# Message passing on one Trainium2 core: SyncE fetches four of 391 pairs of edge tiles per layer row by row, and the gather ring goes from 20 slots to 16

## What is computed

```python
ew = edge_attr @ edge_w + edge_b
for l in range(3):
    residual = x
    msg = relu(x[src] * ew)
    out = 0
    for i in range(3):                       # three types of edges
        h = segment_sum(msg * (edge_type == i), dst, n)
        out = out + (h * inv_cnt[i]) @ weights[l, i]
    out = out + x @ roots[l] + biases[l]
    x = residual + relu(out)
return layernorm(x0 + x)
```

## Time and profile before

| | us |
|---|---|
| time, median of 3 runs | 3607.24 (3604.1 to 3611.32) |
| the profiled execution's own time | 3611.26 |
| its span, first to last instruction | 3609.5 |
| mean granted TensorE clock | 0.846 of 2.4 GHz |
| busy: PE, DVE, ACT, POOL | 2854.7, 2139.7, 1204.2, 2232.8 |
| layer 0, 1, 2 by their first and last `collect` | 23 to 1232, 1248 to 2421, 2429 to 3597 |

### The profile page before, as it was taken

How to read it: one execution, slowest core, us unless ns; L and a number is a source line. 1 busy time by engine, 2 the same in 40 slices (tenths; PEclk the granted TensorE clock), 3 DMA queues, 4 the chain that set the end, 5 groups by cost and what they waited for, 6 DMA issues and landing times.

```text
span 3609.5 us, 57851 instructions
## 1 busy us (share of the span) xinstructions
PE 2854.7 (79%) x17654; PEld 2646.3 (73%) x17654; DVE 2139.7 (59%) x6079; ACT 1204.2 (33%) x2542; POOL 2232.8 (62%) x2363
## 2 busy tenths in 40 slices
PE   6888887888888777878778778877877777787887
PEld 5777777777777676777777777777777777777776
DVE  5666666666666555555555555555555565656656
ACT  4555555555544322222222222222222222222222
POOL 6666666666666566666666666656666666666664
PEclk8788888898888878788888988887888888888888
DMA  6555555555555444444444444444444444444443
GB/s 171 153 158 152 156 156 158 150 158 160 152 158 158 125 133 122 125 132 122 129 129 125 131 125 131 128 126 130 123 124 126 127 127 128 129 126 127 127 128 97
DMA packets 313363, 491.03 MB, mean 136 GB/s; under 512 B 62115, under 2 KB 200030, under 8 KB 313054
## 3 DMA queue, kind: packets, MB, share of 16 engines
q0 software_dynamic: 112608, 307.65, 30.1%
q1 hardware_dynamic: 199628, 179.45, 16.9%
q10 hardware_dynamic: 818, 0.18, 0.0%
HBM read 429.61 MB, written 57.43 MB: 135 GB/s over the span
## 4 chain that ended last, share of the span: by engine, by line
PE 59%; issue 19%; DVE 11%; another core or an unknown queue 8%; DVEq 3%; DMA 0%; ACT 0%; ACTq 0%
PE bank L973 29%; PE bank L929 16%; PE bank L1018 12%; DVE acc L1195 5%; DVE xg L1369 2%; PE bank L994 1%; DVEq L1339 1%; DVEq L1195 1%; DVE t L1212 1%; DVE t L1251 1%; PE bank L965 0%; DVEq L306 0%; DVE t L1224 0%; DVE S L1154 0%
## 5 line engine op out<-in xcount | busy, mean ns | idle before, releaser
L781 POOL DMA_INDIRECT xg<-x,idx x1540 | 1466.0, 952 | 868.3 <-issue 385.0
L1369 DVE TENSOR_TENSOR xg<-xg,bank 128x512 f32<-128x512 f32 x1170 | 802.7, 686 | 1373.8 <-remote 785.5
L973 PE MATMUL bank<-S,xg 128*128 128x96 f32 x9384 | 1522.8, 313 | 101.6 <-issue 92.6
L973 PEld LDWEIGHTS bank<-S,xg 128*128 128x128 f32 x9384 | 1434.2, 228 | 150.2 <-issue 120.0
L863 ACT ACTIVATE xg<-xg 128x512 f32<-128x512 f32 x1170 | 736.8, 630 | 1855.0 <-issue 1070.1
L929 PE MATMUL bank<-wsb,at 128*128 128x256 f32 x4692 | 1008.8, 344 | 386.7 <-issue 240.9
L929 PEld LDWEIGHTS bank<-wsb,at 128*128 128x128 f32 x4692 | 772.0, 228 | 442.1 <-issue 358.1
L781 POOL DMA_INDIRECT xg<-in_x_dram,idx x782 | 741.7, 948 | 465.3 <-issue 181.4
L1195 DVE TENSOR_TENSOR acc<-acc,bank 128x192 f32 x2346 | 816.1, 348 | 46.0 <-issue 14.8
L1018 PE MATMUL bank<-W,acc 128*128 128x256 f32 (+1 forms) x1764 | 532.8, 422 | 36.0 <-issue 34.3
L1018 PEld LDWEIGHTS bank<-W,acc 128*128 128x128 f32 (+1 forms) x1764 | 399.0, 263 | 51.9 <-issue 40.1
(11 more groups left out here) (72 smaller groups left out, 613.9 us busy)
## 6 DMA issues: line engine op xcount, KB each, us to landing
at<-attr_t SPq DMA_DIRECT2D x585, 128.0 KB
attr_t<-hs SPq DMA_DIRECT2D x196, 128.0 KB
xg<-x,idx POOLq DMA_INDIRECT x1540
hs<-in_attr_q_dram SPq DMA_DIRECT2D x196, 64.0 KB
xg<-in_x_dram,idx POOLq DMA_INDIRECT x782
x<-t SPq DMA_DIRECT2D x96, 128.0 KB
xblk<-x SPq DMA_DIRECT2D x96, 128.0 KB
y<-t SPq DMA_DIRECT2D x94, 128.0 KB
```

The source lines that it names most:

```text
L781: eng.indirect_dma_start(out=xg[:, n % XR, :], out_offset=None, in_=rows_in, in_offset=bass.IndirectOffsetOnAxis(ap=rows_at, axis=0)).then ...
L973: last = eng.matmul(sums_bank(l, q, i)[:, 192 * i + 96 * h:192 * i + 96 * h + 96], xg[:, n % XR, 128 * h:128 * h + 128], S[:, slot(l, 2 * ...
L1369: eng.tensor_tensor(v, v, shared_bank("edges", l, q)[:, :].rearrange("p (i d) -> p i d", i=2), ALU.mult).then_inc(s_m, 1)
```

## The change

In each layer four of the 391 pairs (steps 103, 197, 290 and 384, `by_row`) are not gathered by GpSimd any more. SyncE fetches their rows: it loads eight node numbers at a time from a small table `rown` into registers and issues one DMA of one row for each of the 256 edges of a pair, 1024 a layer, 3072 in all. They are spread evenly over steps 10 to 377 (2.78 rows a step) and stand at the end of each step, behind that step's other DMAs. The rows go to an own buffer `xr` of two pairs (`RB`), the semaphores `s_row` count them, and the first row of a pair waits until the pair that used the buffer before has been summed. To make room the ring `xg` goes from 20 slots to 16: a gather now waits for the pair eight places earlier among those gathered. VectorE waits for one semaphore instead of two at a fetched pair. Nothing is changed in the work of TensorE, VectorE and ScalarE but the places that they read and write.

The core of the diff:

```diff
-    XR, SR, TR, AR = 20, 8, 3, 6
+    XR, SR, TR, AR = 16, 8, 3, 6
...
+    RB, ROW0, ROW1 = 2, 10, 384
+    by_row = [ROW0 + (ROW1 - ROW0) * (i + 1) // 4 for i in range(4)]
...
+        xr = sb("xr", [128, 2 * RB, D])
+        rown = sb("rown", [128, 128], I32)
...
+        def gathered(Q):
+            return Q // NP * (NP - len(by_row)) + Q % NP - sum(p < Q % NP for p in by_row)
+        in_ring = [Q for Q in range(L * NP) if Q % NP not in by_row]
...
+            def load_row_numbers():
+                for i, p in enumerate(by_row):
+                    a = 128 * tile(2 * p)
+                    eng.dma_start(rown[32 * i:32 * i + 2, :], src[a:a + 256].rearrange("(q p) -> q p", q=2)).then_inc(s_rn, 16)
...
+            def fetch_rows(l, a, b):
+                for r in range(a, b):
+                    i, m = divmod(r, 256)
+                    if r == 0 and l == 0:
+                        eng.wait_ge(s_rn, 16 * len(by_row))
+                    if m == 0 and (l or i >= RB):
+                        u = i - RB if i >= RB else i - RB + len(by_row)
+                        eng.wait_ge(s_sc, collected(l if i >= RB else l - 1, by_row[u]))
+                    if m % 8 == 0:
+                        _, vals = nc.values_load_multi_w_load_instructions(
+                            rown[32 * i + m // 128:32 * i + m // 128 + 1, m % 128:m % 128 + 8], engines=[SP], min_val=0, max_val=N - 1,
+                            skip_runtime_bounds_check_because="a source is a node's number")
+                        numbers.update({m % 256 + j: v for j, v in enumerate(vals)})
+                    eng.dma_start(xr[m % 128:m % 128 + 1, 2 * (i % RB) + m // 128, :],
+                                  xs[l][bass.ds(numbers.pop(m), 1), :]).then_inc(s_row[i % RB], 16)
+            def row_of(q):
+                return min(4 * 256, max(0, 4 * 256 * (q - ROW0) // (ROW1 - 6 - ROW0)))
...
                         for k in starting(q, late):
                             store(l, k)
+                        fetch_rows(l, row_of(q), row_of(q + 1))
...
             def gather(l, j):
-                n = l * NT + j
-                if n >= XR:
-                    eng.wait_ge(s_sc, collected(*divmod((n - XR) // 2, NP)))
+                G = gathered(l * NP + j // 2)
+                c = 2 * G + j % 2
+                if c >= XR:
+                    eng.wait_ge(s_sc, collected(*divmod(in_ring[G - XR // 2], NP)))
...
                     for j in range(2 * AHEAD, NT):
-                        gather(l, j)
+                        if j // 2 not in by_row:
+                            gather(l, j)
```

More of the change, by code:

```diff
@@ L209, in gnn_program @@
         s_g = sems("s_g", XR)
+        s_rn = sem("s_rn")
+        s_row = sems("s_row", RB)
         s_e, s_m, s_r, s_S, s_sc, s_acc = (sem(n) for n in ("s_e", "s_m", "s_r", "s_S", "s_sc", "s_acc"))
@@ L268, in reload_step, with rows_of, tile_rows, fetched @@
             return max(2 * g - 5, keep_step(g) + 1)
+        def gathered(Q):
+            return Q // NP * (NP - len(by_row)) + Q % NP - sum(p < Q % NP for p in by_row)
+        in_ring = [Q for Q in range(L * NP) if Q % NP not in by_row]
+        def rows_of(Q):
+            if Q % NP in by_row:
+                c, ring_of = 2 * (by_row.index(Q % NP) % RB), xr
+            else:
+                c, ring_of = 2 * gathered(Q) % XR, xg
+            return ring_of[:, c:c + 2, :]
+        def tile_rows(n):
+            return rows_of(n // 2)[:, n % 2, :]
+        def fetched(l, i):
+            return 16 * 256 * (l * (len(by_row) // RB) + i // RB + 1)
+        def wait_rows(eng, n):
+            l, q = divmod(n // 2, NP)
+            if q in by_row:
+                i = by_row.index(q)
+                eng.wait_ge(s_row[i % RB], fetched(l, i))
+            else:
+                c = 2 * gathered(n // 2) + n % 2
+                eng.wait_ge(s_g[c % XR], 16 * (c // XR + 1))
+        assert all(AHEAD <= p < NP - 1 and tile(2 * p) + 1 < NT - 1 for p in by_row)
         def starting(q, lag):
@@ L686, in _ @@
             keep_attr(0)
+            def load_row_numbers():
+                for i, p in enumerate(by_row):
+                    a = 128 * tile(2 * p)
+                    eng.dma_start(rown[32 * i:32 * i + 2, :], src[a:a + 256].rearrange("(q p) -> q p", q=2)).then_inc(s_rn, 16)
+            SP = mybir.EngineType.SP
+            numbers = {}
+            def fetch_rows(l, a, b):
[15 more added lines that the diff above has]
+                return min(4 * 256, max(0, 4 * 256 * (q - ROW0) // (ROW1 - 6 - ROW0)))
             def load_sources(l):
@@ L722, in fast @@
                                 load_x0(1)
+                        if l == 0 and q == 0:
+                            load_row_numbers()
                         if l == 0 and q in (1, 3, 5, 7):
@@ L781, in gather @@
                 eng.indirect_dma_start(
-                    out=xg[:, n % XR, :], out_offset=None, in_=rows_in,
-                    in_offset=bass.IndirectOffsetOnAxis(ap=rows_at, axis=0)).then_inc(s_g[n % XR], 16)
+                    out=xg[:, c % XR, :], out_offset=None, in_=rows_in,
+                    in_offset=bass.IndirectOffsetOnAxis(ap=rows_at, axis=0)).then_inc(s_g[c % XR], 16)
             eng.wait_ge(s_src0, 32)
@@ L854, in fast @@
                             eng.wait_ge(s_m1, l + 1)
-                            v = xg[:, (2 * Q) % XR, :]
+                            v = tile_rows(2 * Q)
                             eng.activation(v, v, ACT.Relu).then_inc(s_r1, 1)
                             eng.wait_ge(s_m, Q + 1)
-                            v = xg[:, (2 * Q + 1) % XR, :]
+                            v = tile_rows(2 * Q + 1)
                             eng.activation(v, v, ACT.Relu).then_inc(s_r, 1)
@@ L861, in fast @@
                             eng.wait_ge(s_m, Q + 1)
-                            v = xg[:, (2 * Q) % XR:(2 * Q) % XR + 2, :]
+                            v = rows_of(Q)
                             eng.activation(v, v, ACT.Relu).then_inc(s_r, 1)
@@ L973, in collect @@
                         last = eng.matmul(sums_bank(l, q, i)[:, 192 * i + 96 * h:192 * i + 96 * h + 96],
[L974 removed]
+                                          tile_rows(n)[:, 128 * h:128 * h + 128], S[:, slot(l, 2 * q + i), :],
                                           start=True, stop=True)
@@ L1179, in first_rows @@
             def first_rows(l, q):
-                v = xg[:, (2 * (l * NP + q)) % XR:(2 * (l * NP + q)) % XR + 2, :]
+                v = rows_of(l * NP + q)
                 n = AHEAD * (l - 1) + q + 1
@@ L1355, in fast @@
                             for i in range(2):
-                                n = 2 * Q + i
-                                eng.wait_ge(s_g[n % XR], 16 * (n // XR + 1))
-                                v = xg[:, n % XR, :]
+                                wait_rows(eng, 2 * Q + i)
+                                v = tile_rows(2 * Q + i)
                                 eng.tensor_tensor(v, v, shared_bank("edges", l, q)[:, 256 * i:256 * i + 256],
@@ L1361, in fast @@
                         elif 0 <= q < NP:
-                            for i in range(2):
-                                n = 2 * Q + i
-                                eng.wait_ge(s_g[n % XR], 16 * (n // XR + 1))
+                            for i in range(1 if q in by_row else 2):
+                                wait_rows(eng, 2 * Q + i)
                             if l and q < AHEAD:
```

1 line of the change is left out of this document (removed).

## The result

The changed kernel is slower: 3730.0 us (3726.79 to 3740.9, 4 runs) against 3609.28 us (3604.1 to 3615.49, 4 runs), a ratio of 1.0338 with a 95% interval of 1.0326 to 1.035. The prediction said 3593 us. Its span is 3725.0 us, 115.5 more than before.

What follows compares the result with a forecast made beforehand. GpSimd's gathers, with late news of TensorE's sums, were taken to set the pace. Terms of -25, +8 and +3 us made -14: 3593 us for the median, likeliest range 3580 to 3600 (0.50), wide range 3572 to 3665.

Steps and rivals of the forecast that it cites:

- I take 0.62: SyncE's one-row DMAs: each takes 0.62 us with its load and register work, bounds 0.35 and 0.85 us.
- SyncE keeps up: SyncE in layer 0: rows and other work fill 5.4 of 6.18 us in two steps, 87%.
- break-even points: SyncE's price per row at which two steps are full: 0.77 us in layer 0, 0.93 in layers 1 and 2.
- I put in 3 us: Layer 0: SyncE's odd steps begin late at times and TensorE waits for reloaded edge attributes, 3 us more.
- -25: GpSimd at the 12 fetched pairs: two gathers fewer save 2.1 us each, 25 us less, bounds 0 and 36.
- +8: Ends of the three layers: the smaller ring leaves eight fast pairs instead of ten, 8 us more, bounds 0 and 8.
- The second rival: SyncE in layer 0: at 0.85 us a row it is too slow and bounds the kernel, about 3678 us; chance 0.09.
- gathers in flight delay the news: Middle of a layer: TensorE's increments reach other engines late during gathers; GpSimd's gathering sets 2.99 us a pair.
- nothing paces but the three banks: TensorE's banks set the pace, removed gathers bring 0: 3609 us; chance 0.20, shared with gain and losses cancelling.
- rows burden the DMAs: DMA engines: rows lengthen each pair's pause by up to 0.136 us, 150 us in all, up to 3743 us; chance 0.04.

Runs made afterwards that it cites:

- e13: Kernel before with ring of 16; layer 1 rows from fixed addresses, layer 2 register rows, no gathers from its pair 196: 3385.4 us beside 3576.21.
- e3: Changed kernel with SyncE's rows from fixed addresses, without number loads and register work: 2943.79 us, 0.9919 of the kernel before.
- e2: Changed kernel without SyncE's rows and its loads of node numbers, the four pairs fetched by nobody: 2942.89 us, 0.9915 of the kernel before.
- e1_ring16: Kernel before with a gather ring of 16 slots in place of 20, everything gathered: 2973.43 us beside 2968.2, ratio 1.0019.
- e7_after: The changed kernel itself, unaltered, on another chip: 2979.66 us beside 2967.13 for the kernel before, ratio 1.0035.
- e6: Kernel before without GpSimd's gathers from pair 196 of layer 2 on: 2.49 us a pair with gathers, 1.93 without.
- e5: Changed kernel without GpSimd's gathers from pair 196 of layer 2 on, SyncE's rows kept: 2.45 us a pair, then 1.98.

## Why the prediction was wrong, point by point

**The step that failed** is "I take 0.62" for a row, between 0.35 and 0.85 us all in, and with it "SyncE keeps up". The neighbours it was read from the earlier trace rows were plain DMAs, one instruction each, and one load in an idle stretch. Measured, a row with its share of the loads occupies SyncE for 0.83 us in layer 0 and 0.96 us in layer 1, the latter over the upper bound too. The prediction's own break-even points were 0.77 and 0.93 us, so SyncE is over both. With 2.05 and 0.84 us of other work in two steps (counted: 1.9 and 0.8) two steps take it 5.57 x 0.83 + 2.05 = 6.7 and 5.57 x 0.96 + 0.84 = 6.2 us; observed are 6.6 and 6.1, against 6.17 and 6.00 before. (An engine that never pauses must come out at the length of the steps; that SyncE hardly pauses is shown by its waits above.) Over the 184 double steps of a layer the longer steps make 184 x (6.59 - 6.17) = 77 us in layer 0, 184 x (6.11 - 6.00) = 20 us in layer 1 and 184 x (6.14 - 6.01) = 24 us in layer 2, 121 us in all, and 121 were measured. In the prediction's sum this sits in the term "I put in 3 us" for the late SyncE: with its other two terms, -25 and +8, that term came to about 138 us. I had added 0.09 us for the loads and the register work to the price of a DMA, as if two more instructions were almost free; on a late chip each costs 0.3 us.

**The second rival** (SyncE too slow) was the right mechanism, with the right sign and place; it was given 0.09 and priced at 3678 us, with layers 1 and 2 held safe. It should have had far more: the range of a row's price, 0.35 to 0.85 us, straddled the break-even of 0.77 us, and above that each 0.1 us costs 1024 x 0.1 = 102 us a layer, while below it nothing more is gained.

**What held.** That gathers in flight delay the news and set the pace on a late chip: 2.26 against 0.01 us and 3.00 against 1.96 us a pair in e13, which also refutes "nothing paces but the three banks". That 24 gathers are worth 25 us: 30.5 us on prompt chips, about 8 us for 8 in one layer of a late one. That the ring costs up to 8 us: 5 to 6 us on prompt chips; on a late one it wasn't separated. That rows burden the DMAs is refuted for a prompt chip by e3 beside e2, 0.9 us apart, and layer 1 of e13 shows no such loss on a late one; single rows may sit on few DMA engines, but it cost nothing that these runs can tell. Nor do rows hold the news back further: the increments are no later in the changed kernel.

**What the rows could not tell, and what I overlooked.** The 0.47 us from start to start and the twelve in a run come from an engine that waits most of the time, and its trace gives no warning: 9 of 588 reloads (L653) take over 0.65 us, the longest 1.74 us, and in e1_ring16 on a prompt chip it is 17, the longest 2.39 us. What stood in the rows was the late news. I read the late news as a matter of TensorE's increments alone and did not ask whether another engine would be held back by the same gathers; the part of the change that was new was exactly on such an engine.

**Left open.** Why gathers in flight hold back SyncE's instructions and TensorE's increments on some chips and not on others, and what passes more slowly there. A low clock is not it: between 2008 and 2014 us, where VectorE waits 3.15 us for the news, TensorE's granted clock was 1.00. Whether VectorE's and ScalarE's increments are late too can't be said: those recorded come 0.01 us after the end in the median of VectorE's sums and ScalarE's relus, but in layer 1 of the kernel before a third to a half of them have no record. The Trainium skill ("Runtime: NRT & Kernel Launch", section "Instruction fetch mechanics") says that each sequencer streams its instructions by itself and that this stays hidden behind the rate of issue. A price per instruction, whatever its kind, is what one would see if it did not stay hidden while gathers are in flight. The profile shows transfers of instructions (its queues q8 and q14), and they speak against it as far as they go: in layer 1 of the changed kernel there are 111 of them beside 801 stalls, and they take no longer than on a prompt chip (medians 0.97 and 0.36 us on the late one, 0.97 and 0.39 in e7_after). How instructions get from there to SyncE no run shows. Nor was a version with fewer rows measured on a late chip; by the sum above two pairs would need 5.57 / 2 x 0.83 + 2.05 = 4.4 of 6.2 us there, which leaves room for a small gain.

## What to carry to other kernels

Before work goes to an idle queue, multiply its instructions, every register operation included, by their price when they follow each other closely beside the kernel's other traffic, and compare with the time in a step. The trace of a queue that mostly waits gives only a lower bound of that price (here 0.56 us against 0.83 to 0.96), so try it in a small kernel, on more than one chip. If the price range straddles the break-even, forecast the loss, since the gain is bounded and the loss is not. Cut instructions before moving work: on a late chip one instruction a row cost 0.36 us where three cost 0.91 to 0.93. And fill such a queue by stage: on a prompt chip the same rows that lost 30 us in layer 0 gained 10 in layer 1, and two pairs in layer 0 with four in the others beat both kernels.

## What the runs showed of the hardware

The same program takes 2968 us on four chips and 3572 to 3609 us on two others and in the measurement; TensorE's granted clock was 0.92 (ring of 16) on the former and 0.85 on the latter. With no gathers in flight a pair takes 1.93 and 1.98 us on prompt chips (e6, e5) and 1.96 us on a late one (e13). While indirect gathers are in flight on a chip of the slower kind, SyncE's closely following instructions, of any kind, meet stalls of 0.7 us (400 at the 514 rows of three instructions each in e13, none at the 469 without gathers), and TensorE's increments come 2.3 to 2.7 us late on average in the kernel before and in e13, against 0.05 us or less in e1 on a prompt chip. On such a chip a one-row DMA of 1 KB costs SyncE 0.23 us in the instruction, 0.33 us from start to start from a fixed address and 0.43 with its address from a register, and 3072 of them hold up nothing else.
